# A Mamba-style block beside an FFN in fp32: W_out's columns one slot sooner, another list of sums handed over, the FFN's first output column in steps of 2, 4 and 5 tiles

## The chip, the cores and the metric

The kernel runs on one core of one Trainium2 chip. It is written in a low-level language in which each engine has its own instruction list in program order and waits on counting semaphores: PE (TensorE, matrix products), DVE (VectorE), ACT (ScalarE), POOL (GpSimd), and SP, which here only issues DMA transfers. The metric is the device time of one execution in microseconds. The time given for the kernel before is the median of three runs; the profile is one more execution with a time of its own.

## The reference

Four sequences (batches) of 512 tokens with 512 channels, all in fp32. A Mamba-style branch and a gated FFN read the same normed input, and their product is added to the input. With the scan's width D = 1024, N = 16 states for each channel, a step size of rank R = 32 and an FFN width of 1376:

```python
xn = _layernorm(x)
proj = xn @ W_in.T
u, gate = jnp.split(proj, 2, axis=-1)
u = silu(depthwise_causal_conv(u, conv_w) + conv_b)        # 4 taps
dt, Bm, Cm = jnp.split(u @ Wx.T, [R, R + N], axis=-1)      # each _rmsnorm'ed
delta = softplus(dt @ Wdt.T + dt_bias)
# for every token:
dA = exp(delta[..., None] * A)
state = dA * state + (delta * u)[..., None] * Bm[:, None, :]
y = einsum('bdn,bn->bd', state, Cm)
s = ((y + u * D_param) * silu(gate)) @ W_out.T
g = silu((silu(xn @ w_gate.T) * (xn @ w_up.T)) @ w_down.T)
out = x + s * g
```

## The kernel before

**Units and slots.** The four sequences run one after the other, b = 0 to 3. The scan of a sequence has 32 units, one for each state n and each half of the channels, and each unit two slots, so a sequence has 64 slots. In slot s:

- POOL makes dBu for two channel tiles, one product of 128x1024 (L913), up to three slots ahead of its reader;
- ACT makes two tiles of dA = exp(delta * A) (L673);
- DVE runs the two scans of 128x512 (L1191), and then adds into y the states of the unit before, weighted with C (L1107), two token tiles c in each slot: c = 0, 1 in an even slot, c = 2, 3 in an odd one;
- PE transposes the states of unit s // 2 (L1554, two token tiles, four blocks each) into two banks hT, as soon as the scans are done, then does a small transposition of other data where there is one, and then one column of matrix products.

A bank hT is free once the sum that reads it is made. DVE reads it itself (L1107), or the sum is handed over: ACT scales the tile (`take_state`, L779) and POOL adds it in (`add_part`, L866). `handed_over(u, first)` lists the tiles c given away for each unit u; `first` is True for sequence 0.

**Columns.** The columns of a sequence are laid out in tables by slot number. Slots 0 to 21 hold the FFN's gate and up projections (four slots sooner in sequences 1 to 3), then come the second half of W_in's gate, then, in sequences 1 to 3, the product with W_out of the sequence before: 8 columns from slot `S_OUT` on, two for each of the four output tiles e (L1464). The first of them waits for the gated values of this sequence (`sg_done`, DVE L1016), since its bank was the gate's. Two slots after each pair DVE multiplies with the FFN's result (`scale_g`, L1025), and from slot 32 on PE transposes these results back (L1372) and DVE adds them to the residual (L1152). From slot 31 on stand W_in's u columns of the next sequence (`U_AT`, L1252), and between them the FFN's down projection (`DOWN_AT`, L1498): four output tiles of 11 products t = 0 to 10 each, the first of them in three steps at slots 33, 36 and 39. fp32 products have two records for each t in the trace, so 8 records are four t.

**Loads.** SP loads the weights of L1464 and L1498 into a ring of two buffers, 512 KB at a time, in a fixed list that `load_order` makes: a buffer that is used up is loaded again when PE has signalled the last product that reads it (`dn_ps` after t = 3, 7 and 10). One buffer of w_down holds eight t. In sequence 0 the two buffers are still shared with W_in's u columns up to here, in the order U0, DOWN0, U0+1, DOWN0+1: DOWN0 (t = 0 to 7) and DOWN0+1 (t = 8 to 10 of tile 0, and on) lie in the same buffer. In sequences 1 and 2 they lie in the two buffers side by side. In sequence 3 the down projection has another form, which the change leaves alone.

**POOL's list.** Beside dBu and the handed sums POOL makes the step sizes delta (`step_size`, L843), the scan's inputs delta * u (`inputs`, L848, 128x1024 each), in sequence 0 the low parts of split weights (`rest_w`, L831, each waiting for ACT's rounding, L520), the powers of the norms (L815 and L826) and the products with the gate (L852). Each stands at a fixed slot. `inputs(b+1, 0)` of the next sequence waits for DVE's step sizes (L1177) and stands in slot 61, behind that slot's dBu and ahead of the one made in slot 62.

## Time and profile before

| | us |
|---|---|
| median of 3 runs (1109.97 to 1112.58) | 1111.97 |
| profiled execution | 1112.61 |
| its span | 1110.8 |
| PE busy | 1024.4 |
| DVE busy | 1035.5 |
| POOL busy | 967.4 |
| ACT busy | 719.0 |

The profiled execution is 0.64 us over the median. Its span runs from the first to the last instruction; 1.8 us lie outside it. The mean granted TensorE clock is 0.972 of full speed. In a timeline a row is: start, duration, engine, source line, operation, tiles written and read, sizes, and in brackets the idle time just before it with the engine whose work ended it. DVE's slot 0 of the four sequences starts at about 64, 335, 594 and 852 us.

### The profile page before, as it was taken

What the parts mean: (1) busy time and instruction counts of PE and PEld (TensorE: products, weight loads), DVE (VectorE), ACT (ScalarE), POOL (GpSimd) and SP (SyncE); (2) the same over time, 40 slices, a digit from 0 to 9 for tenths busy, and PEclk for the clock granted to TensorE, in tenths of its full rate; (3) what the DMA queues carried; (4) which work ended last, traced back from release to release, by engine and by line L of the source; (5) the groups of instructions that cost most, each with busy time, mean ns of one, the idle gap of its engine ahead of it and who ended that gap; (6) DMA issues with size and microseconds to landing.
All of it is one profiled execution on the core that took longest, in us unless ns stands there. A gap on an engine that the chain in (4) does not pass through costs nothing.

```text
span 1110.8 us, 14875 instructions
## 1 busy us (share of the span) xinstructions
PE 1024.4 (92%) x5040; PEld 753.5 (68%) x5040; DVE 1035.5 (93%) x1237; ACT 719.0 (65%) x1177; POOL 967.4 (87%) x531
## 2 busy tenths in 40 slices
PE   6969988899989999999999999998998999999877
PEld 5848766666758886675857887576766888555444
DVE  4679999899899999999999999999999999999995
ACT  4666766777576877477676786477576685456540
POOL 3648998999989999779979999968998999979981
PEclk9879999799989999999999999999999999999989
DMA  4626754443324654343233564334332543335511
GB/s 148 224 97 217 258 196 172 153 161 109 104 88 151 224 181 151 115 161 124 97 120 111 184 217 157 133 123 142 125 109 93 183 163 138 114 114 170 167 42 57
DMA packets 46619, 160.93 MB, mean 145 GB/s; under 512 B 5358, under 2 KB 5614, under 8 KB 37072
## 3 DMA queue, kind: packets, MB, share of 16 engines
q1 hardware_dynamic: 46400, 159.93, 42.2%
q8 instruction: 40, 0.66, 0.2%
q14 instruction: 35, 0.29, 0.1%
q10 hardware_dynamic: 144, 0.07, 0.0%
HBM read 135.59 MB, written 24.38 MB: 144 GB/s over the span
## 4 chain that ended last, share of the span: by engine, by line
PE 31%; POOL 28%; DVE 22%; issue 15%; ACT 3%; DMA 1%; SPq 0%; DVEq 0%; POOLq 0%
POOL sb_dBu L913 17%; DVE sb_h L1191 12%; PE pj L1252 10%; PE pj L1464 7%; PE hT L1554 6%; POOL sb_yT L866 6%; DVE sb_yT L1107 5%; DVE sb_un L989 2%; POOL sb_v L848 2%; PE pj L1572 2%; POOL sb_u L852 1%; PE pj L1498 1%; PE pj L1257 1%; PE pj L1529 1%; POOL sb_w_sp L831 1%
## 5 line engine op out<-in xcount | busy, mean ns | idle before, releaser
L913 POOL TENSOR_TENSOR sb_dBu<-sb_v,sb_bb 128x1024 f32<-128x1024 f32 x254 | 603.8, 2391 | 41.3 <-DVE sb_h L1191 28.5
L1191 DVE TENSOR_TENSOR_SCAN sb_h<-dA,sb_dBu 128x512 f32<-128x512 f32 x512 | 597.1, 1209 | 18.7 <-POOL sb_dBu L913 15.5
L673 ACT ACTIVATE dA<-sb_delta,sb_apar 128x512 f32<-128x512 f32 x510 | 344.9, 689 | 221.8 <-DVE sb_h L1191 219.9
L1252 PE MATMUL pj<-sb_x_hi,sb_w_sp 128*128 128x512 f32 x1208 | 344.6, 409 | 21.7 <-DVE sb_un L989 12.2
L1554 PEld LDWEIGHTS hT<-sb_ident,sb_h 128*128 128x128 f32 x2048 | 240.2, 144 | 127.3 <-issue 45.6
L1554 PE MATMUL hT<-sb_ident,sb_h 128*128 128x128 f32 x2048 | 283.5, 280 | 43.8 <-DVE sb_yT L1107 35.1
L1252 PEld LDWEIGHTS pj<-sb_x_hi,sb_w_sp 128*128 128x128 f32 x1208 | 223.2, 193 | 69.7 <-DVE sb_un L989 8.7
L1107 DVE SCALAR_TENSOR_TENSOR sb_yT<-hT,sb_cs,sb_yT 128x512 f32<-128x512 f32 x336 | 238.6, 735 | 10.0 <-PE hT L1554 9.4
L866 POOL TENSOR_TENSOR sb_yT<-sb_yT,sb_part 128x512 f32<-128x512 f32 x140 | 181.1, 1293 | 25.3 <-ACT sb_part L779 25.3
L1252 PE MATMUL pj<-sb_x_lo,sb_w_sp 128*128 128x512 f32 x604 | 167.3, 400 | 0.0
L779 ACT ACTIVATE sb_part<-hT,sb_cs_act 128x512 f32<-128x512 f32 x140 | 95.6, 683 | 95.4 <-PE hT L1554 85.3
L1252 PEld LDWEIGHTS pj<-sb_x_lo,sb_w_sp 128*128 128x128 f32 x604 | 117.1, 194 | 27.3
L1498 PE MATMUL pj<-sb_S,sb_ring 128*128 128x512 f32 x264 | 120.2, 593 | 0.0
L1464 PE MATMUL pj<-sb_u,sb_ring 128*128 128x512 f32 x192 | 86.6, 594 | 0.0
L1498 PEld LDWEIGHTS pj<-sb_S,sb_ring 128*128 128x128 f32 x264 | 47.9, 190 | 43.5 <-issue 43.0
L989 DVE SCALAR_TENSOR_TENSOR sb_un<-pj,sb_cw,sb_un 128x511 f32<-128x511 f32 (+2 forms) x93 | 69.5, 747 | 4.9 <-ACT sb_un L549 2.7
L831 POOL TENSOR_TENSOR sb_w_sp<-sb_ring,sb_w_sp 128x1024 fp32r<-128x1024 f32 x21 | 49.9, 2380 | 25.5 <-ACT sb_w_sp L520 25.3
L1464 PEld LDWEIGHTS pj<-sb_u,sb_ring 128*128 128x128 f32 x192 | 34.7, 191 | 35.0 <-issue 35.0
L852 POOL TENSOR_TENSOR sb_u<-sb_u,sb_sgate 128x512 f32<-128x512 f32 x32 | 41.1, 1288 | 8.5 <-DVE sb_u L1022 8.5
L848 POOL TENSOR_TENSOR sb_v<-sb_delta,sb_un 128x1024 f32<-128x1024 f32 x14 | 33.5, 2395 | 14.8 <-DVE sb_delta L1177 14.8
L1529 PE MATMUL pj<-sb_ring,sb_S 128*128 128x512 f32 x88 | 39.8, 593 | 0.0
L837 POOL TENSOR_TENSOR sb_un<-sb_v,sb_un 128x512 f32<-128x512 f32 x30 | 38.5, 1289 | 0.0
(148 smaller groups left out, 774.4 us busy)
## 6 DMA issues: line engine op xcount, KB each, us to landing
sb_w_sp<-w_cache SPq DMA_DIRECT2D x55, 1024.0 KB, 4.8
sb_ring<-w_ring SPq DMA_DIRECT2D x67, 512.0 KB, 3.6
sb_bb<-b_rows SPq DMA_DIRECT2D x128, 256.0 KB, 3.4
w_cache<-sb_w_sp SPq DMA_DIRECT2D x19, 1024.0 KB, 4.9
sb_xio<-x SPq DMA_DIRECT2D x7, 1024.0 KB, 7.6
out<-sb_xio SPq DMA_DIRECT2D x3, 1024.0 KB, 5.6
sb_xio<-x SPq DMA_DIRECT2D x4, 256.0 KB, 3.3
out<-sb_xio SPq DMA_DIRECT2D x4, 256.0 KB, 2.0
```

The lines of the kernel that those rows point to most:

```text
L673: nc.scalar.activation(dA[g % 2][:, :], delta[:, j, :], ACT.Exp, scale=apar[:, j, n:n + 1]).then_inc(dA_done, 1)
L779: nc.scalar.activation(dst, hT[c % H_BANKS][:, :], ACT.Copy, scale=cs_act[:, c, n:n + 1]).then_inc(ev_done, 1)
L831: nc.gpsimd.tensor_tensor(w_lo[:, buf], ring[:, slot], w_hi[:, buf].bitcast(fp32), ALU.subtract).then_inc(lo_done, 1)
L866: nc.gpsimd.tensor_tensor(y, y, part[:, (len(acts) - q) % 2, :], ALU.add).then_inc(yp_done, 1)
L913: nc.gpsimd.tensor_tensor(dBu[:, dbu_buffer(s), :, :], v[:, j:j + 2, :], bb[:, i % B_RING, :].unsqueeze(1).to_broadcast([P, 2, T]), ALU.mu ...
L989: nc.vector.scalar_tensor_tensor(out=acc[:, k:T], in0=bank[:, 0:T - k], scalar=cw[:, j, KC - 1 - k:KC - k], in1=acc[:, k:T], op0=ALU.mult, ...
L1107: nc.vector.scalar_tensor_tensor(out=y, in0=hT[c % H_BANKS][:, :], scalar=cn, in1=y, op0=ALU.mult, op1=ALU.add).then_inc(y_done, 1)
L1191: nc.vector.tensor_tensor_scan(h[:, i % 2, 2 * part + e, :], dA[g % 2][:, :], dBu[:, dbu_buffer(s), e, :], 0.0, ALU.mult, ALU.add).then_in ...
L1252: done = nc.tensor.matmul(bank[:, :], w[:, kk * P:(kk + 1) * P], xs[:, kk, :], start=(p == 0), stop=(p == len(products) - 1))
L1464: done = nc.tensor.matmul(pj[e % 2][:, :], ring[:, slot_of(b, OUT0 + e), part, m * P:(m + 1) * P], u[:, j, :], start=(j == 0), stop=(j == ...
L1498: done = nc.tensor.matmul(pj[DOWN_BANK[e]][:, :], ring[:, slot_of(b, DOWN0 + x3 // 2), x3 % 2, t % 4 * P:(t % 4 + 1) * P], S[:, t, :], sta ...
L1554: done = nc.tensor.transpose(hT[c % H_BANKS][:, j * P:(j + 1) * P], h[:, i % 2, j, c * P:(c + 1) * P], ident[:, :])
```

## The change

Four tables and the list of POOL are altered; no instruction is computed otherwise.

```diff
-S_OUT = 23
+S_OUT = 22
-DOWN_AT = {33: (0, range(0, 4)), 36: (0, range(4, 8)), 39: (0, range(8, 11)),
+DOWN_AT = {33: (0, range(0, 2)), 36: (0, range(2, 6)), 39: (0, range(6, 11)),
...
-        return () if u < FIRST_UNIT else (0, 2) if 11 <= u < 23 else (0,)
+        return () if u < FIRST_UNIT else (0, 2) if u < 21 else (0,)
+    if u in (17, 18):
+        return 0, 1, 2
...
-        after["used", OUT0] = "xres"
+        after["used", OUT0 + 1] = "xres"
...
-                    if s == 14:
+                    if s == (17 if first else 14):
                         step_size(b, 2)
-                    if s == 16:
+                    if s == (23 if first else 16):
                         inputs(b, 2)
-                    if s == 18:
+                    if s == (25 if first else 18):
                         step_size(b, 3)
-                    if s == 20:
+                    if s == (27 if first else 20):
                         inputs(b, 3)
...
-                    if s == SLOTS - 3:
+                    if s == SLOTS - 2:
                         inputs(b + 1, 0)
```

The eight W_out columns stand in slots 22 to 29 instead of 23 to 30, `scale_g` in slots 26, 28, 30 and 32. In sequence 0 the sums (21, 2) and (22, 2) go back to DVE, in its slots 45 and 47. In sequences 1 to 3 the sums (17, 1) and (18, 1) are handed over as well, out of DVE's slots 36 and 38. The load of the residual is issued behind the second W_out buffer's reload instead of the first's. POOL makes the second half's step sizes and inputs of sequence 0 later, and the first inputs of the next sequence behind the dBu of slot 62 (in the same slot) instead of ahead of it. Up to line 83 the numbers are alike; behind that they are 2 or 3 higher in the changed kernel.

On PE in sequence 0, slot 39, before: the transpositions of the states (L1554), of y (L1328), then the three products t = 8 to 10, the first of which waits for its weights (w_in0).

```order
390 L1554 MATMUL hT<-sb_ident,sb_h 128x128 [waits y_done]
391 L1554 MATMUL hT<-sb_ident,sb_h 128x128 x3
392 L1328 MATMUL pj<-sb_ident,sb_yT 128x128 [waits yu_done]
393 L1328 MATMUL pj<-sb_ident,sb_yT 128x128 x3
394 L1498 MATMUL pj<-sb_S,sb_ring 128x512 [waits w_in0]
395 L1498 MATMUL pj<-sb_S,sb_ring 128x512 x2
```

The same place in the changed kernel:

```order
390 L1557 MATMUL hT<-sb_ident,sb_h 128x128 [waits y_done]
391 L1557 MATMUL hT<-sb_ident,sb_h 128x128 x3
392 L1331 MATMUL pj<-sb_ident,sb_yT 128x128 [waits yu_done]
393 L1331 MATMUL pj<-sb_ident,sb_yT 128x128 x3
394 L1501 MATMUL pj<-sb_S,sb_ring 128x512 x2
395 L1501 MATMUL pj<-sb_S,sb_ring 128x512 [waits w_in0]
396 L1501 MATMUL pj<-sb_S,sb_ring 128x512 x2
```

The products t = 6 and 7 now stand right ahead of the three that wait for the next weights.

On SP around the same place, before: loads of B's rows (L384), of split weights (L444) and of the ring (L378); the ring's load is the one of DOWN0+1.

```order
71 L444 DMA sb_w_sp<-w_cache 128x2048 [waits u_ps,wc_out1,wc_out0]
72 L384 DMA sb_bb<-b_rows 128x512 [waits dBu_done]
73 L378 DMA sb_ring<-w_ring 128x1024 [waits dn_ps]
74 L384 DMA sb_bb<-b_rows 128x512 [waits dBu_done]
75 L444 DMA sb_w_sp<-w_cache 128x2048 [waits u_ps,wc_out1,wc_out0]
```

In the changed kernel:

```order
71 L446 DMA sb_w_sp<-w_cache 128x2048 [waits u_ps,wc_out1,wc_out0]
72 L386 DMA sb_bb<-b_rows 128x512 [waits dBu_done] x2
73 L446 DMA sb_w_sp<-w_cache 128x2048 [waits u_ps,wc_out1,wc_out0]
74 L380 DMA sb_ring<-w_ring 128x1024 [waits dn_ps]
75 L386 DMA sb_bb<-b_rows 128x512 [waits dBu_done]
```

The ring's load moved behind one load of B's rows and one of split weights.

On PE in sequence 1, slots 22 to 24, before: state transpositions (L1554), transpositions of the next sequence's x (L1228), and the first W_out columns (L1464).

```order
362 L1554 MATMUL hT<-sb_ident,sb_h 128x128 x8
363 L1228 MATMUL pj<-sb_ident,sb_xio 128x128 x8
364 L1554 MATMUL hT<-sb_ident,sb_h 128x128 x8
365 L1464 MATMUL pj<-sb_u,sb_ring 128x512 x4
366 L1554 MATMUL hT<-sb_ident,sb_h 128x128 x8
367 L1228 MATMUL pj<-sb_ident,sb_xio 128x128 x8
368 L1464 MATMUL pj<-sb_u,sb_ring 128x512 x4
```

In the changed kernel:

```order
362 L1557 MATMUL hT<-sb_ident,sb_h 128x128 x8
363 L1231 MATMUL pj<-sb_ident,sb_xio 128x128 x8
364 L1467 MATMUL pj<-sb_u,sb_ring 128x512 x4
365 L1557 MATMUL hT<-sb_ident,sb_h 128x128 x8
366 L1467 MATMUL pj<-sb_u,sb_ring 128x512 x4
367 L1557 MATMUL hT<-sb_ident,sb_h 128x128 x8
368 L1231 MATMUL pj<-sb_ident,sb_xio 128x128 x8
```

The first W_out column stands ahead of slot 23's state transpositions instead of behind them.

On POOL at the turn from sequence 0 to 1, before: dBu (L913), handed sums (L866), and the next sequence's inputs (L848).

```order
119 L866 TENSOR_TENSOR sb_yT<-sb_yT,sb_part 128x512
120 L913 TENSOR_TENSOR sb_dBu<-sb_v,sb_bb 128x1024
121 L848 TENSOR_TENSOR sb_v<-sb_delta,sb_un 128x1024
122 L913 TENSOR_TENSOR sb_dBu<-sb_v,sb_bb 128x1024
123 L866 TENSOR_TENSOR sb_yT<-sb_yT,sb_part 128x512
```

In the changed kernel:

```order
120 L868 TENSOR_TENSOR sb_yT<-sb_yT,sb_part 128x512
121 L915 TENSOR_TENSOR sb_dBu<-sb_v,sb_bb 128x1024 x2
122 L868 TENSOR_TENSOR sb_yT<-sb_yT,sb_part 128x512
123 L850 TENSOR_TENSOR sb_v<-sb_delta,sb_un 128x1024
124 L915 TENSOR_TENSOR sb_dBu<-sb_v,sb_bb 128x1024 x2
```

The inputs moved behind one dBu and one handed sum.

## Rows read from the trace of the kernel before

**Rows 1.** Page, part 1: busy us (share of the span) and instructions of each engine.

```profile
PE 1024.4 (92%) x5040; PEld 753.5 (68%) x5040; DVE 1035.5 (93%) x1237; ACT 719.0 (65%) x1177; POOL 967.4 (87%) x531
```

**Rows 2.** Page, part 5: costliest groups: busy, mean ns of one | idle before, releaser.

```profile
L913 POOL TENSOR_TENSOR sb_dBu<-sb_v,sb_bb 128x1024 f32<-128x1024 f32 x254 | 603.8, 2391 | 41.3 <-DVE sb_h L1191 28.5
L866 POOL TENSOR_TENSOR sb_yT<-sb_yT,sb_part 128x512 f32<-128x512 f32 x140 | 181.1, 1293 | 25.3 <-ACT sb_part L779 25.3
```

**Rows 3.** Waits, whole run: engine, tile, line <- releaser: us in total, times, longest.

```profile
PE hT L1554 <- DVE sb_yT L1107: 35.1, 28, 2.9
```

**Rows 4.** Timeline of DVE, sequence 0: slots 17 and 21.

```profile
139.29 2.34 DVE L1191 TENSOR_TENSOR_SCAN sb_h<-dA,sb_dBu 128x512 f32<-128x512 f32 x2 [0.92 <-POOL sb_dBu L913]
...
158.23 2.34 DVE L1191 TENSOR_TENSOR_SCAN sb_h<-dA,sb_dBu 128x512 f32<-128x512 f32 x2 [1.16 <-POOL sb_dBu L913]
```

**Rows 5.** Timeline of POOL, sequence 0: the dBu of slot 31.

```profile
189.72 2.36 POOL L913 TENSOR_TENSOR sb_dBu<-sb_v,sb_bb 128x1024 f32<-128x1024 f32 x1 [3.86 <-DVE sb_h L1191]
```

**Rows 6.** Timeline of DVE, sequence 0, slots 50 to 55.

```profile
280.62 2.34 DVE L1191 TENSOR_TENSOR_SCAN sb_h<-dA,sb_dBu 128x512 f32<-128x512 f32 x2 [1.84 <-POOL sb_dBu L913]
...
285.40 2.34 DVE L1191 TENSOR_TENSOR_SCAN sb_h<-dA,sb_dBu 128x512 f32<-128x512 f32 x2 [1.20 <-POOL sb_dBu L913]
...
300.89 2.34 DVE L1191 TENSOR_TENSOR_SCAN sb_h<-dA,sb_dBu 128x512 f32<-128x512 f32 x2 [0.62 <-ACT dA L673]
```

**Rows 7.** Timeline of PE, sequence 0, slots 39 and 40.

```profile
241.53 2.74 PE L1498 MATMUL pj<-sb_S,sb_ring 128*128 128x512 f32 x6
244.11 1.04 PE L1554 MATMUL hT<-sb_ident,sb_h 128*128 128x128 f32 x8
```

**Rows 8.** Line 378, 226 to 262 us: the ring's two loads, issue to landing.

```profile
DMA to landing us min/median/max: 3.5/3.6/3.7
```

**Rows 9.** Timeline of DVE, sequence 0, slot 41.

```profile
248.67 0.73 DVE L1107 SCALAR_TENSOR_TENSOR sb_yT<-hT,sb_cs,sb_yT 128x512 f32<-128x512 f32 x1
249.31 2.31 DVE L989 SCALAR_TENSOR_TENSOR sb_un<-pj,sb_cw,sb_un 128x511 f32<-128x511 f32 x3
```

**Rows 10.** Windows: stretch, busy us (instructions) of PE, PEld, DVE, ACT, POOL, then granted clock.

```profile
326.00:331.00 5.00, 5.00 (x16) 4.33 (x17) 4.37 (x6) 3.75 (x5) 5.00 (x3) 0.50 0.00 0
585.00:588.00 3.00, 3.00 (x11) 2.61 (x10) 2.35 (x3) 2.40 (x4) 3.00 (x3) 0.50 0.00 0
...
1022.00:1025.00 3.00, 1.38 (x12) 1.01 (x10) 3.00 (x5) 1.38 (x2) 3.00 (x3) 1.00 0.54 175
```

**Rows 11.** Timeline of PE at the turn to sequence 1.

```profile
325.95 1.94 PE L1554 MATMUL hT<-sb_ident,sb_h 128*128 128x128 f32 x8 [2.92 <-DVE sb_yT L1107]
...
342.42 1.07 PE L1252 MATMUL pj<-sb_x_hi,sb_w_sp 128*128 128x512 f32 x4
...
344.22 1.16 PE L1252 MATMUL pj<-sb_x_hi,sb_w_sp 128*128 128x512 f32 x4
```

**Rows 12.** Timeline of PE at the turn to sequence 3.

```profile
858.45 1.07 PE L1252 MATMUL pj<-sb_x_hi,sb_w_sp 128*128 128x512 f32 x4
...
861.15 1.16 PE L1252 MATMUL pj<-sb_x_hi,sb_w_sp 128*128 128x512 f32 x4 [0.28 <-DVE sb_S L1133]
```

**Rows 13.** Timeline of DVE at the turn to sequence 3.

```profile
856.52 2.34 DVE L1191 TENSOR_TENSOR_SCAN sb_h<-dA,sb_dBu 128x512 f32<-128x512 f32 x2 [0.68 <-POOL sb_dBu L913]
```

**Rows 14.** Timeline of PE, sequence 1, slots 23 and 24.

```profile
430.96 3.67 PE L1464 MATMUL pj<-sb_u,sb_ring 128*128 128x512 f32 x8
434.47 1.04 PE L1554 MATMUL hT<-sb_ident,sb_h 128*128 128x128 f32 x8
```

**Rows 15.** Timeline of DVE, sequence 1, slots 24 to 35.

```profile
430.19 0.68 DVE L1016 SCALAR_TENSOR_TENSOR sb_sgate<-sb_sgate,pj 128x512 f32<-128x512 f32 x1
...
433.08 0.72 DVE L1107 SCALAR_TENSOR_TENSOR sb_yT<-hT,sb_cs,sb_yT 128x512 f32<-128x512 f32 x1
...
474.71 0.69 DVE L1152 TENSOR_TENSOR sb_xio<-sb_xio,pj 128x512 f32<-128x512 f32 x1 [0.65 <-PE pj L1372]
```

**Rows 16.** Timeline of PE, sequence 3, slots 34 and 35.

```profile
986.02 0.66 PE L1372 MATMUL pj<-sb_ident,sb_gT 128*128 128x128 f32 x4 [1.29 <-DVE sb_xio L1152]
```

## The prediction, made before the changed kernel was run

> **What bounds the kernel now.** I read the busy shares first [rows 1]: DVE 93%, PE 92%, POOL 87%. No engine bounds the whole; the three hand buffers to one another, and whichever is last differs from slot to slot. The grouped waits come next [rows 3]: PE waits 35.1 us in 28 places for DVE's sums, since the banks hT are free only when DVE has read them. So a term of the change is worth what it moves at its own slot, minus what the next engine then says. The timelines of the slots that the change touches are the rest of the reading. All sums are made against the profiled execution, 1112.61 us, which is 0.64 over the median of the runs, 1111.97.
>
> **Sequence 0, POOL's list in the first half.** DVE waits for dBu in slots 17, 19 and 21; the first and the last are 0.92 and 1.16 us [rows 4]. The four moved operations are as large as a dBu (128x1024), 2.39 us each [rows 2]. With the first ones gone from slots 14 to 20, the three waits, about 3.1 us with the middle one taken as the mean, go. But the work has to be done before slot 32, and three of the four pieces, 7.2 us, now stand in slots 23 to 27. POOL's only idle time there is 3.86 us [rows 5]. The excess, 7.2 - 3.86 = 3.3 us, less the lead that DVE's earlier arrival doesn't leave it, returns as waits in slots 26 to 28. Followed row by row (dBu, rest of a split weight after ACT's rounding, a moved piece, in their new order) slot 29 starts 0.8 us sooner than now. Ends: 0 if POOL eats all of it, -3.1 if none. I take **-0.8**, as the excess is near the gain.
>
> **Sequence 0, two sums back to DVE.** POOL makes two additions of 1.29 us less [rows 2], 2.58 us, ahead of slots 50 and 51, where DVE waits 1.84 and 1.20 us for dBu, and ahead of slot 55, where it waits 0.62 us for ACT [rows 6], which in turn stands behind POOL's powers there. DVE takes over two sums; each moves its next instruction on by 0.64 us (248.67 to 249.31) [rows 9], 1.3 in all. The two waits are 3.04 us against POOL's 2.58 plus DVE's own 1.3 of delay, so both go. -3.04 - 0.62 + 1.3 = **-2.4**; ends -1.3 (only POOL's 2.58) and -2.4.
>
> **Sequence 0, steps of 2, 4 and 5 tiles.** The three products t = 8 to 10 begin at 241.53 [rows 7], with weights that were loaded when t = 7 in slot 36 had freed their buffer. The order shows that t = 7 is now the second product of slot 39, right ahead of t = 8, and that both buffers' loads are the same buffer. So t = 6 and 7 end at 241.53 + 2 x 0.91 = 243.4 (2.74 for three is 0.91 each [rows 7]); SP issues the load then and it lands 3.6 us later [rows 8], at 247.0; three products of 2.6 us follow, and the transpositions behind them, of which the first tile takes half of 1.04, are ready at 250.7. Their reader on DVE is the next slot's sum, now at 248.67 [rows 9]: a stall of **2.0 us**. PE idles 3.6 us for it. In the trace PE's granted clock is 0.50 for the 5 us from 326 and the 3 us from 585, both behind idle times of near 2.9 us [rows 10, 11], 1.2 in place of 2.4 GHz; at 1022 to 1025, where PE was idle half of the time in smaller pieces, it stayed 1.00 [rows 10]. An idle time of 3.6 is nearer to the first kind. Three us at half clock lose 1.5 us of work, five lose 2.5; the next columns in slots 40 to 44 are full ones with DVE close behind. I add 1.7, in all **+3.7**; ends +2.0 (clock stays) and +5.2. In sequences 1 and 2 the two buffers are loaded side by side, beforehand, and nothing happens.
>
> By the Trainium skill's page "DMA: Bandwidth & Descriptors" (Anatomy of one DMA) a transfer takes 2.0 us plus its bytes over 436 GB/s, which is 3.2 us for 512 KB as an estimate; the trace has 3.5 to 3.7 [rows 8], and by the page the stall would be 1.6 instead of 2.0. By "TensorE: Matmul & The Clock Gate" (Part 1) the array runs at half rate once it has sat idle and has to be busy again to get it back; the trace agrees behind both idle times of 2.9 us [rows 10, 11], and this speaks against the change, since a load in front of PE would then cost more than its wait.
>
> Sequence 0 together: -0.8 - 2.4 + 3.7 = **+0.5**.
>
> **The turns, inputs behind one dBu.** DVE waits 0.68 us for dBu in slot 1 before sequence 3 [rows 13] and as much in slot 62, because POOL's inputs, which wait for DVE, have the dBu of slot 62 behind them. With that dBu ahead these waits, 1.3 us at each of three turns, go. At the turn to sequence 1 nothing follows: PE is dense from 325.95 on, at half clock first, and its columns come 1.80 us apart (342.42 to 344.22) without idle time [rows 11]; DVE meets PE's transpositions again some ten slots on. At the turns to 2 and 3 PE's column waits for DVE's product with the FFN's gate: 858.45 to 861.15 is 2.70 us [rows 12], where a dense pair takes 1.80. So 0.9 to 1.0 comes back at each. I take **-0.95 twice, -1.9**; ends 0 and -1.3 for each.
>
> **W_out one slot sooner, sequences 1 and 2.** The first W_out column needs the gated values that DVE makes at 430.19 to 430.87 in slot 24 [rows 15], and begins at 430.96 already [rows 14]. One slot sooner in the list it can't begin sooner, but the transpositions of slot 23 now stand behind its 3.5 us instead of ahead of it. DVE's sum at 433.08 [rows 15] has to wait until the first tile is out at 434.47 + 1.04 = 435.5 [rows 14], 2.4 us. Followed slot by slot, DVE is 2.5 us late at slot 26, up to 4.9 at slots 31 and 33, and once the columns end a slot sooner 3.5 us come back in slot 30 and two of its own waits for PE vanish: the addition to the residual at 474.71 [rows 15] comes at 476.7. **+2.0**; ends +0.9 (PE has only one block of transpositions more to do behind 430.96, 434.47 to 435.35) and +2.7. From there DVE is last, and the two sums handed over in slots 36 and 38 save it 2 x 0.64 = **-1.3**; POOL has nothing to lose there. Net **+0.7** in each, +1.4.
>
> **Sequence 3.** The start of W_out is bound the same way and its last column ends where it does now. Behind it stand no columns of a next sequence: PE waits for DVE already, 1.29 us at 986.02 [rows 16]. DVE has one slot more to do between the last column and the residual, so the tail's down projection begins one DVE slot later, by 3.3 us. From there to about 1022 PE bounds. PE's idle time grows from 1.29 to about 3 us, again the kind behind which the clock fell [rows 10, 11]: between 0.3 and 3.4, I take +1.5. The handed sums save only 0.3 here. +3.3 + 1.5 - 0.3 = **+4.5**.
>
> **Sum.** 0.5 - 1.9 + 1.4 + 4.5 = +4.5; 1112.6 + 4.5 = **1117.1 us**.
>
> **Rivals.** (a) *No change: the clock holds.* All mechanisms as above, but behind neither idle time does the clock fall: the 1.7 and the 1.5 that I added for it go, 4.5 - 3.2 = +1.3, 1113.9 us. For it: smaller idle times at 1022 to 1025 left the clock at 1.00 [rows 10]. Against: both of 2.9 didn't. Chance 0.22. (b) *Faster: W_out's early column costs nothing.* If DVE's and PE's slack between slots 24 and 36 takes the 2.4 us in (DVE waits for PE there already, 0.65 at 474.71 [rows 15]), so that the column freed at slot 30 is a gain, S_OUT gives 0 in sequences 1 to 3: the sum loses 2.0 + 2.0 + 3.3 + 1.5 = 8.8 and gives -4.3, 1108.3 us; with the load's stall hidden too, -8.0, 1104.6 us. It decides at the point where slot 35's residual addition starts no later, relative to slot 24, than now. Against it: PE is dense from 430.96 to that place. Chance 0.12. (c) *Slower than forecast.* Both clocks stay down for the long spell and POOL's list gives nothing back: (5.2 - 3.7) + (3.4 - 1.5) + 0.8 = 4.2 more, 1121.3 us. Chance 0.16. My own case, within 1.5 us of 1117.1, has 0.5.
>
> **How the numbers follow.** 0.3% of 1112 is 3.3 us, about what a measurement of this kernel can tell from no change. Faster by more than that is case (b), 0.12. Slower by more is my case for nearly all of it, 0.42, and (c), less a little for offsetting errors: 0.55. The rest, 0.33, is (a) and the lower edge of mine. The range takes (a), mine and nearly all of (c), and reaches to the slower part of (b): 1109.5 to 1121.5 us.
>
> **What would show it.** In the changed profile: DVE's waits for POOL at slots 17, 19, 21, 50, 51 and at the three turns gone; a PE idle time of some 3.6 us before the third product of slot 39 in sequence 0, released by a ring load, and a granted clock of 0.50 behind it; in sequences 1 and 2 a DVE wait of about 2.4 us for hT in slot 25, and the residual's additions 2 us later relative to the first W_out column; in sequence 3 the tail's down projection 3.3 us later behind that column. I am wrong if the ring's load lands before t = 8 needs it, if the first W_out column begins sooner than DVE's gate in slot 24 (then S_OUT is a gain), or if DVE has slack in the slots 24 to 35 that I took for none.

## The result, and the profile after

| | before | changed |
|---|---|---|
| median, us | 1112.58 (7 runs, 1105.41 to 1114.66) | 1118.18 (7 runs, 1116.82 to 1120.68) |
| profiled execution, its span | 1112.61, 1110.8 | 1118.18, 1116.4 |
| mean granted clock | 0.972 | 0.972 |

The ratio is 1.0058 with a 95% interval of 1.004 to 1.0076: 0.6% slower, clear of no change. The forecast was 1117.1 us in a range of 1109.5 to 1121.5, with slower as the likeliest case at 0.55.

The page of the changed kernel, part 1 (the busy shares, as [rows 1]), and three of the grouped waits of the whole run (the first answers to [rows 3]):

```profile
PE 1023.5 (92%) x5040; PEld 752.9 (67%) x5040; DVE 1033.0 (93%) x1233; ACT 718.9 (64%) x1181; POOL 972.6 (87%) x535
```

```profile
PE hT L1557 <- DVE sb_yT L1110: 34.3, 23, 2.9
...
DVE sb_yT L1110 <- PE hT L1557: 26.4, 24, 4.9
...
DVE sb_h L1194 <- POOL sb_dBu L915: 8.3, 10, 1.5
```

The engines do the same work but for a few sums that changed hands between DVE and POOL. What changed is who waits: before, DVE waited 15.5 us in 18 places for POOL's dBu, the idle time that page part 5 lists ahead of the scans, and 9.4 us for PE's transpositions. Now it is 8.3 us for POOL and 26.4 us for PE, with one wait of 4.9 us. So 7 us were taken off POOL's account and 17 put on PE's.

How much of it reached the end is read from the start of DVE's scans slot by slot, changed minus before. This difference is called the lag (positive is later). Behind slot 4 of sequence 0 it moves at these places, and elsewhere by 0.2 us or less:

| place | lag goes from, to | moved | forecast |
|---|---|---|---|
| sequence 0, slots 16 to 29 (POOL's list) | 0.0, -1.0 | -1.0 | -0.8 |
| sequence 0, slots 42 to 43 (steps 2, 4, 5) | -1.0, +4.0 | +5.0 | +3.7 |
| sequence 0, slots 43 to 55 (two sums to DVE) | +4.0, +1.3 | -2.7 | -2.4 |
| turn to sequence 1 | +1.5, 0.0 | -1.5 | 0 |
| sequence 1, slots 25 to 36 (W_out) | 0.0, +2.3 | +2.3 | +2.0 |
| sequence 1, slots 36 to 39 (handed sums) | +2.3, +0.9 | -1.3 | -1.3 |
| turn to sequence 2 | +0.9, -0.1 | -1.0 | -0.95 |
| sequence 2, slots 25 to 39 | -0.1, +0.8 | +0.9 | +0.7 |
| turn to sequence 3 | +0.8, -0.7 | -1.5 | -0.95 |
| sequence 3, slots 25 to 40 (W_out, sums) | -0.7, +2.8 | +3.5 | +4.5 |
| sequence 3, slots 40 to 51 | +2.8, +4.1 | +1.3 | none |
| sequence 3, slot 51 to the end | +4.1, +5.6 | +1.5 | none |

**Sequence 0, slot 39.** PE's timeline of the changed kernel, then SP's:

```profile
240.53 1.88 PE L1501 MATMUL pj<-sb_S,sb_ring 128*128 128x512 f32 x4
246.05 5.49 PE L1501 MATMUL pj<-sb_S,sb_ring 128*128 128x512 f32 x6 [3.63 <-DMA sb_ring<-w_ring]
251.33 1.25 PE L1557 MATMUL hT<-sb_ident,sb_h 128*128 128x128 f32 x8
```

```profile
239.48 0.32 SPq L446 DMA_DIRECT2D sb_w_sp<-w_cache  x1
242.45 0.33 SPq L380 DMA_DIRECT2D sb_ring<-w_ring  x1
```

The load is issued when t = 7 is done (242.4) and PE stands still for 3.63 us until it lands; the forecast had 3.6. The three products then take 5.49 us, where they took 2.74 before [rows 7]: the clock. The same place by windows (busy us of PE, PEld, DVE, ACT and POOL, then the granted clock):

```profile
246.00:249.00 3.00, 2.95 (x4) 1.41 (x5) 1.72 (x2) 0.00 (x0) 3.00 (x2) 0.50 0.16 59
249.00:252.00 3.00, 3.00 (x8) 1.34 (x8) 0.00 (x0) 0.00 (x0) 0.26 (x1) 0.54 0.00 0
252.00:255.00 3.00, 3.00 (x18) 2.54 (x17) 2.32 (x4) 2.82 (x5) 2.06 (x2) 1.00 0.00 0
```

1.2 in place of 2.4 GHz for nearly 6 us, and DVE stands idle for 4.9 us of it: its sum, at 248.67 before [rows 9], has this wait in DVE's timeline:

```profile
252.61 0.76 DVE L1110 SCALAR_TENSOR_TENSOR sb_yT<-hT,sb_cs,sb_yT 128x512 f32<-128x512 f32 x1 [4.90 <-PE hT L1557]
```

**Sequence 1, slots 22 to 25.** PE's and DVE's timelines of the changed kernel, to be held against [rows 14, 15]:

```profile
427.38 1.04 PE L1231 MATMUL pj<-sb_ident,sb_xio 128*128 128x128 f32 x8
430.91 3.67 PE L1467 MATMUL pj<-sb_u,sb_ring 128*128 128x512 f32 x8 [2.49 <-issue]
434.42 1.04 PE L1557 MATMUL hT<-sb_ident,sb_h 128*128 128x128 f32 x8
435.29 3.60 PE L1467 MATMUL pj<-sb_u,sb_ring 128*128 128x512 f32 x8
```

```profile
430.13 0.68 DVE L1019 SCALAR_TENSOR_TENSOR sb_sgate<-sb_sgate,pj 128x512 f32<-128x512 f32 x1
...
435.49 0.75 DVE L1110 SCALAR_TENSOR_TENSOR sb_yT<-hT,sb_cs,sb_yT 128x512 f32<-128x512 f32 x1 [2.39 <-PE hT L1557]
```

The first W_out column begins at 430.91, behind DVE's gate (430.13 + 0.68), as it did before at 430.96. It is put down to "issue", but it is that gate: the column follows it by 0.1 us in both kernels. PE stands idle for 2.49 us ahead of it with slot 23's transpositions behind it in its list, and DVE waits 2.39 us for them (2.4 in the forecast).

**The turns.** DVE's wait for dBu at 856.52 [rows 13] is gone, and PE's column at the turn to sequence 3, at 861.15 before [rows 12], is here:

```profile
858.39 1.07 PE L1255 MATMUL pj<-sb_x_hi,sb_w_sp 128*128 128x512 f32 x4
859.30 1.03 PE L1557 MATMUL hT<-sb_ident,sb_h 128*128 128x128 f32 x8
860.39 1.17 PE L1255 MATMUL pj<-sb_x_hi,sb_w_sp 128*128 128x512 f32 x4
```

858.39 to 860.39 is 2.00 us, before it was 2.70.

**Sequence 3, slots 34 to 36.** PE's timeline: the state transpositions that now wait for a DVE sum, and the first column of the tail's down projection, which began at 986.52 before:

```profile
985.45 1.79 PE L1557 MATMUL hT<-sb_ident,sb_h 128*128 128x128 f32 x8 [2.92 <-DVE sb_yT L1110]
...
989.76 3.60 PE L1532 MATMUL pj<-sb_ring,sb_S 128*128 128x512 f32 x8
```

It begins 3.2 us later although the last W_out column begins 0.7 us sooner (976.33, before 977.06), so it is 4.0 us later behind that column. The forecast had 3.3 us and up to 3.4 for the clock.

**Sequence 3, slot 51.** DVE's timeline has a wait there that the kernel before didn't have:

```profile
1045.75 2.34 DVE L1194 TENSOR_TENSOR_SCAN sb_h<-dA,sb_dBu 128x512 f32<-128x512 f32 x2 [1.22 <-POOL sb_dBu L915]
```

### The profile page after: what moved, and what is told of

The parts are those of the page before. It is cut to its first block, busy times and chain, and to the rows that moved or that the text cites. A ratio compares the mean times of both kernels' runs of the same rounds, so it can differ in the third digit from the quotient of the medians.

```text
span 1116.4 us, 14880 instructions
## 1 busy us (share of the span) xinstructions
PE 1023.5 (92%) x5040; PEld 752.9 (67%) x5040; DVE 1033.0 (93%) x1233; ACT 718.9 (64%) x1181; POOL 972.6 (87%) x535
## 4 chain that ended last, share of the span: by engine, by line
PE 55%; DVE 23%; issue 11%; POOL 8%; ACT 2%; DMA 1%; SPq 0%; DVEq 0%; POOLq 0%; ACTq 0%
PE pj L1255 26%; PE hT L1557 12%; DVE sb_h L1194 12%; PE pj L1467 7%; DVE sb_yT L1110 5%; POOL sb_dBu L915 4%; PE pj L1501 3%; DVE sb_un L992 3%; PE pj L1575 2%; POOL sb_yT L868 2%; PE pj L1260 2%; POOL sb_w_sp L833 1%; PE pj L1597 1%; DVE sb_u L1025 1%; PE pj L1331 1%
## 5 line engine op out<-in xcount | busy, mean ns | idle before, releaser
L1110 DVE SCALAR_TENSOR_TENSOR sb_yT<-hT,sb_cs,sb_yT 128x512 f32<-128x512 f32 x332 | 235.6, 735 | 27.2 <-PE hT L1557 26.4
L868 POOL TENSOR_TENSOR sb_yT<-sb_yT,sb_part 128x512 f32<-128x512 f32 x144 | 185.0, 1287 | 25.8 <-ACT sb_part L781 25.8
L1501 PE MATMUL pj<-sb_S,sb_ring 128*128 128x512 f32 x264 | 123.1, 604 | 3.6 <-DMA sb_ring<-w_ring 3.6
```

Of the source, the lines that this page charges most:

```text
L868: nc.gpsimd.tensor_tensor(y, y, part[:, (len(acts) - q) % 2, :], ALU.add).then_inc(yp_done, 1)
L1110: nc.vector.scalar_tensor_tensor(out=y, in0=hT[c % H_BANKS][:, :], scalar=cn, in1=y, op0=ALU.mult, op1=ALU.add).then_inc(y_done, 1)
L1501: done = nc.tensor.matmul(pj[DOWN_BANK[e]][:, :], ring[:, slot_of(b, DOWN0 + x3 // 2), x3 % 2, t % 4 * P:(t % 4 + 1) * P], S[:, t, :], sta ...
```

## The experiments

Twelve kernels were run. "Lag" is always DVE's scan start against the kernel before, slot by slot as in the table above. Only its moves from one slot to another are used, so that the start of the program, which differs by up to 6 us from one execution to the next, drops out. W_out's columns and the steps were run alone and taken out alone. POOL's list, the two sums of sequence 0 and the turns were never run alone: their terms are told apart by the place at which the lag moves, and in the two kernels that keep all three as they were (W_out alone, steps alone) DVE's waits at those places are about as long as before.

**W_out back in its old slots**, and with it the load of the residual, which goes back behind the first reload in every kernel that has W_out in slots 23 to 30.

```diff
-S_OUT = 22
+S_OUT = 23
```

> The changed kernel with only W_out's columns put back into slots 23 to 30 (and the residual's load behind the first reload, as before). Theory: the early column can't begin before DVE's gate of slot 24, so the transpositions of slot 23 queue behind it; in the changed profile that cost 2.3 us in each of sequences 1 and 2 up to slot 36, and 3.5 us in sequence 3. Undone, the three losses go: about 8 us less than the changed kernel, -2.5 us against the kernel before (+5.6 - 8.1), ratio near 0.998; DVE's wait of 2.4 us for hT in slot 25 is gone. Rival: the loss in these slots comes from the handed sums or the residual's load, then the time stays near +5 us and the wait stays.

Measured: 1107.81 us, ratio 0.9963 (0.995 to 0.9975). In sequences 1 and 2 the lag stays flat from slot 9 to 36, DVE's wait in slot 25 is gone, and the two handed sums then give 1.3 us in each. In sequence 3 it loses 1.7 us at slots 26 to 28 instead of 3.5: the clock was at 0.57 from 942 to 945 us in this execution, around the first W_out column. In the medians the kernel is 10.4 us faster than the changed one. W_out accounts for 2.3 us in each of sequences 1 and 2 and the difference of 3.5 and 1.7 in sequence 3, which is more than the 5.6 us that the whole change costs; a shorter half clock behind the stall of slot 39 (3.6 instead of 5.0 us) and in the tail is in the 10.4 too.

**One slot sooner, alone on the kernel before.**

```diff
-S_OUT = 23
+S_OUT = 22
```

> The kernel before with one part of the change alone: W_out's columns in slots 22 to 29 (and the residual's load behind the second reload). Theory: the loss doesn't need the other parts. DVE waits about 2.4 us for hT in slot 25 of sequences 1 and 2, slot 36 starts 2.3 us later relative to slot 25, nothing of it comes back since DVE has no wait for POOL between slot 36 and the turn, but the turn's two waits for POOL (0.65 and 0.70) can take nothing in either, as they move along; sequence 3 is 3.5 us longer to slot 34 and keeps it. In all +8 us, ratio 1.0072. Rival (the early column is harmless by itself, the handed sums or POOL's list made it late): under +2 us.

Measured: 1123.58 us, ratio 1.0118 (1.0089 to 1.0146), more than I expected. Sequence 1 loses 2.2 us, sequence 3 3.5 up to slot 34, both as expected. In sequence 2 it is 3.9. PE's timeline there:

```profile
691.53 5.37 PE L1464 MATMUL pj<-sb_u,sb_ring 128*128 128x512 f32 x8 [2.50 <-issue]
696.73 1.04 PE L1554 MATMUL hT<-sb_ident,sb_h 128*128 128x128 f32 x8
```

The idle time of 2.50 us is the one of 2.49 in the changed kernel's sequence 1. There the column behind it took 3.67 us at full clock, here 5.37 at a granted clock of 0.66 (691 to 694). The early column costs 2.3 us, or 3.9 when the clock falls behind it. Of the 18 early first columns in the six kernels with W_out in slots 22 to 29, four ran at half clock (5.2 to 5.4 us); in the changed kernel's profile none did. No wait of DVE for the residual's load shows in this kernel.

**The first column behind slot 23's transpositions.** W_out's first two columns are issued together in slot 23.

```diff
-                    e, part = (s - S_OUT) // 2, (s - S_OUT) % 2
-                    if 0 <= e < KH and not first:
+                    for q in () if s == S_OUT else (0, 1) if s == S_OUT + 1 else (s - S_OUT,):
+                        e, part = q // 2, q % 2
...
```

> The changed kernel, but W_out's first column is issued in slot 23, behind that slot's transpositions and ahead of the second column; the other columns stay in slots 24 to 29. Theory (the loss in sequences 1 and 2 starts with slot 23's transpositions queueing behind a column that itself waits for DVE): DVE's wait in slot 25 is gone, slot 26 is late by 0.5 to 0.9 us instead of 2.4, and slot 36 by 1.4 instead of 2.3. In sequence 3 the loss is of another kind (DVE has one slot more to do between the last column and the residual) and stays at 3 to 3.5 us up to slot 34. In all 2 to 2.5 us less than the changed kernel, ratio 1.003 to 1.004. Rival (it is PE's total work behind DVE's gate that counts, not its order): slot 36 stays 2.3 us late.

Measured: 1113.02 us, ratio 1.0011 (0.9988 to 1.0034), 5 us less than the changed kernel where 2 to 2.5 were expected. Up to slot 36 of sequences 1 and 2 it is as expected: no wait in slot 25, slot 26 not late at all, 1.1 us of wait for hT in slot 26, and slot 36 late by 1.4. The lag at slot 34 of sequence 3 grows by 2.7 us. So the order gives back 0.9 us in each sequence. The rest of the gain isn't one term: the profiled execution (1114.74) is only 3.4 us below the changed kernel's; in it the stall of sequence 0 cost 3.5 instead of 5.0, but POOL's list gave nothing (see the part on the prediction). The ten executions spread from 1108.39 to 1119.78, and what separates the median from them isn't explained. The cause of the loss in sequences 1 and 2 is the order, for 0.9 of the 2.3 us. That the other 1.4 are one slot's transpositions that PE has to fit in is my reading and not tested.

**Steps of 4, 4 and 3 again.**

```diff
-DOWN_AT = {33: (0, range(0, 2)), 36: (0, range(2, 6)), 39: (0, range(6, 11)),
+DOWN_AT = {33: (0, range(0, 4)), 36: (0, range(4, 8)), 39: (0, range(8, 11)),
```

> The changed kernel with only the steps of 4, 4 and 3 products put back. Theory: the wait of 3.6 us for the ring's load in sequence 0, slot 39, goes, with the half clock behind it: slot 43 starts 5.0 us sooner. Second question: in the changed profile DVE's waits for POOL in slots 50 and 51 were gone, and POOL had had the 5 us of the stall to run ahead. If the two additions taken from POOL suffice alone, slot 56 starts 5.0 us sooner too, +0.6 us against before in all; if it was the stall that let POOL catch up, 0.5 to 3 us of the waits at slots 50 and 51 come back, and the total is +1 to +3.5 us.

Measured: 1113.70 us, ratio 1.0019 (1.0 to 1.0038). The lag doesn't move between slots 42 and 43, and DVE's waits at slots 50 and 51 stay away: the lag falls by 2.5 us up to slot 55 (2.7 in the changed kernel). So the two sums taken from POOL suffice without the stall. In this execution too the first W_out column of sequence 2 ran at half clock (5.37 us) and cost 3.9 instead of 2.3.

**Steps of 2, 6 and 3.** `36: (0, range(2, 8))`, so that t = 6 and 7 are in slot 36.

> The changed kernel with steps of 2, 6 and 3 products: the first step is the changed one, but t = 6 and 7 are in slot 36. Theory (what counts is how long before t = 8 the product t = 7 is made, not the size of the first step): no wait for the ring's load, slot 43 as with 4, 4 and 3 within 0.5 us plus what the longer column of slot 36 costs (two products more, 1.8 us, of which DVE's wait in slots 37 and 38 takes 0 to 1.8). Rival (the load is late for another reason, behind the other loads that moved ahead of it): PE waits over 1 us for the load here too.

Measured: 1113.34 us, ratio 1.0014 (0.9995 to 1.0034), no wait for the load. PE's timeline:

```profile
221.86 5.32 PE L1501 MATMUL pj<-sb_S,sb_ring 128*128 128x512 f32 x12
...
236.46 2.74 PE L1501 MATMUL pj<-sb_S,sb_ring 128*128 128x512 f32 x6
```

The longer column costs nothing (the lag moves by 0.1 us or less from slot 36 to 43). It is the place of t = 7, not the size of the first step. (This execution is 0.7 us behind the one with steps of 4, 4 and 3 at slot 43, but it was so at slot 36 already, by a wait for ACT that two kernels with other steps have as well.)

**Steps of 2, 5 and 4.** `36: (0, range(2, 7))`, so that only t = 7 stands ahead of t = 8.

> The changed kernel with steps of 2, 5 and 4 products: only t = 7 and behind it t = 8 to 10 are in slot 39. Theory: t = 7 ends 0.9 us sooner than in the changed kernel, so the load is issued and lands 0.9 us sooner; PE's idle time in front of t = 8 is again 3.6 us, the clock falls again, and the stall to slot 43 is 5.0 - 0.9 = 4.1 us. If the clock doesn't fall this time it is 2.0 - 0.9 = 1.1 us. Rival (the load's landing time is set by the load of split weights ahead of it): it lands at the same time as in the changed kernel, the idle time grows to 4.5 us and the stall stays 5.0.

Measured: 1118.90 us, ratio 1.0055 (1.0041 to 1.0069); the stall to slot 43 is 3.3 us, smaller than both. Two things differ. The load is issued 2.1 us behind the load of split weights instead of 3.0, and it takes 4.0 us from issue (243.82) to the product (247.82): 0.4 of the 0.9 us is lost, in the direction of the rival. That it is lost behind the load of split weights is likely but not shown by one run. And the half clock was shorter. PE's timeline:

```profile
247.82 4.46 PE L1501 MATMUL pj<-sb_S,sb_ring 128*128 128x512 f32 x6 [4.04 <-DMA sb_ring<-w_ring]
```

4.46 for the three products, against 5.49 in the changed kernel and 2.74 at full clock.

**The steps alone on the kernel before.**

> The kernel before with one part alone: steps of 2, 4 and 5 products. Theory: the wait of 3.6 us for the ring's load appears in slot 39 of sequence 0, slot 43 starts 3.3 to 5.0 us later (the spread is the length of the half clock behind it). But POOL runs on meanwhile, and DVE's waits for it at slots 50 and 51 (1.84 and 1.20) are there to be taken in: 3.0 of it comes back, and the part alone costs only +0.3 to +2.0 us, ratio 1.0003 to 1.0018. So the parts don't add up: in the changed kernel the two sums given back to DVE had already used those waits. Rival (POOL is held up by the stall as DVE is): the waits stay and the cost is +3.3 to +5.0.

Measured: 1116.10 us, ratio 1.0029 (1.0009 to 1.0048). The stall is 3.6 us, and my theory fell: the waits for POOL stayed. DVE's timeline:

```profile
285.29 2.34 DVE L1191 TENSOR_TENSOR_SCAN sb_h<-dA,sb_dBu 128x512 f32<-128x512 f32 x2 [1.64 <-POOL sb_dBu L913]
...
290.07 2.34 DVE L1191 TENSOR_TENSOR_SCAN sb_h<-dA,sb_dBu 128x512 f32<-128x512 f32 x2 [1.20 <-POOL sb_dBu L913]
```

The rival was right: POOL is held up by the stall as DVE is. Its timeline:

```profile
253.91 1.30 POOL L866 TENSOR_TENSOR sb_yT<-sb_yT,sb_part 128x512 f32<-128x512 f32 x1 [2.18 <-ACT sb_part L779]
...
258.62 1.31 POOL L866 TENSOR_TENSOR sb_yT<-sb_yT,sb_part 128x512 f32<-128x512 f32 x1 [1.05 <-ACT sb_part L779]
```

The handed sums in POOL's list need a tile that ACT scales from a bank hT, which PE fills late, and POOL takes its list in order: it stood idle for 3.2 of the 3.6 us. It began the dBu of slot 43 11.9 us ahead of its scan (8.3 before), since that one stood ahead of the stalled sums, but the one of slot 46 9.1 against 8.8. The parts add up after all.

**Sums 17 and 18 back on DVE.** The two lines `if u in (17, 18): return 0, 1, 2` are taken out of the changed kernel.

> The changed kernel with the sums (17, 1) and (18, 1) of sequences 1 to 3 back on DVE. Theory: in sequences 1 and 2 DVE is last behind slot 36 and pays 0.65 us twice in each, +2.6 us. In sequence 3 POOL had only 2.5 us of lead at slot 51 before the change, so the 2.6 us of two more additions came back there as a DVE wait of 1.22 us: that wait is gone, and slot 51 stands 0 to 0.6 us sooner relative to slot 35 than in the changed kernel. In all +2.1 us against the changed kernel, ratio to before about 1.007. Rival: the wait at slot 51 comes from the shifted tail (S_OUT) and stays; then +3.3 us.

Measured: 1121.46 us, ratio 1.0081 (1.006 to 1.0102). The wait at slot 51 of sequence 3 is gone and the lag flat from 37 to 51, while sequences 1 and 2 no longer get their 1.3 us back. The median is 3.3 us over the changed kernel's, the rival's number, but the rival's mechanism (the wait stays) is refuted; in this execution the first W_out column of sequence 3 ran at half clock (5.22 us, 1.5 us more of lag) and the stall of slot 39 cost 3.9 instead of 5.0. DVE's timeline around slot 51:

```profile
1044.68 0.72 DVE L1108 SCALAR_TENSOR_TENSOR sb_yT<-hT,sb_cs,sb_yT 128x512 f32<-128x512 f32 x1
1045.33 2.33 DVE L1192 TENSOR_TENSOR_SCAN sb_h<-dA,sb_dBu 128x512 f32<-128x512 f32 x2
```

**Both parts back: W_out in slots 23 to 30, steps of 4, 4 and 3.**

> The changed kernel with W_out's columns back in slots 23 to 30 and the first output column back in steps of 4, 4 and 3; what is left are POOL's list, the inputs at the turns and the handed sums. Theory: the terms add up. From the runs before: sequence 0 gives -1.0 and -2.5, the turns -1.5 each less up to 0.6 of half clock, the handed sums -1.3 in sequences 1 and 2 and +0.6 in sequence 3: -8 us, near 1104.3 us, ratio 0.9925 (the run with only W_out back less its own stall of 3.6 us). Rival (DVE and PE take the gains back from one another once the stalls are out): -3 to -4 us, ratio 0.997.

Measured: 1105.24 us, ratio 0.9935 (0.991 to 0.9961). What is left of the change makes the kernel faster by 0.65%, near the 0.9925 expected; the rival's 0.997 lies outside the interval. From slot 4 of sequence 0 to slot 63 of sequence 3 the lag falls by 6.0 us in all; sequence 3 has given back 1.7 at slots 27 and 28 (the clock, as in the first run) and 1.3 at slot 51 by then.

**The same with sums 17 and 18 on DVE.**

> As the run before it (W_out and the steps back), and the sums (17, 1) and (18, 1) back on DVE too: only the changes to POOL's list, the turns and sequence 0's sums are left. Theory: +1.3 us in each of sequences 1 and 2, and in sequence 3 DVE's wait at slot 51 gone (-1.2) against 0.65 to 1.3 us more on DVE: +2.1 to +2.7 us against the run before it, ratio to the kernel before 0.9945.

Measured: 1105.48 us, ratio 0.9944 (0.9927 to 0.996). The expected 2.1 to 2.7 us more than the run before it didn't come: the medians differ by 0.2 us, and the two can't be told apart in time. In the traces it is 1.3 us twice against 1.2 at slot 51 and a spell of half clock more or less.

**The same with sums 27 and 28 handed over instead.**

```diff
-    if u in (17, 18):
-        return 0, 1, 2
+    if u in (27, 28):
+        return 0, 1
```

> W_out and the steps back, and instead of (17, 1) and (18, 1) the sums (27, 1) and (28, 1) are handed over in sequences 1 to 3 (DVE's slots 56 and 58, POOL's 58 and 60), where POOL stood idle for 4.9 us in slots 60 and 61 in the kernel before. Theory (a handed sum is free where POOL has idle time before its next use): the same 1.3 us in each of sequences 1 and 2, and no wait at slot 51 of sequence 3: 1 to 1.5 us less than with 17 and 18, near 1103 us. Rival: POOL's inputs at the turn come late behind the added sums and DVE waits in slots 62 or 1; then equal or worse.

Measured: 1106.76 us, ratio 0.9941 (0.9919 to 0.9962), no gain. No wait at slot 51, but new ones in slots 57 (0.8 us) and 59 (1.0 us) of sequences 1 and 2, more than the 1.3 us that the handed sums save. They aren't POOL's. The one of slot 59:

```profile
564.16 2.34 DVE L1194 TENSOR_TENSOR_SCAN sb_h<-dA,sb_dBu 128x512 f32<-128x512 f32 x2 [0.99 <-ACT dA L675]
```

I had looked at POOL's idle time only. A handed sum is also 0.68 us on ACT, which makes dA and has no idle time ahead of slot 59 (softplus of the next sequence and a table load).

**POOL's last two pieces later still**, on top of both parts back.

```diff
-                    if s == (25 if first else 18):
+                    if s == (27 if first else 18):
                         step_size(b, 3)
-                    if s == (27 if first else 20):
+                    if s == (29 if first else 20):
                         inputs(b, 3)
```

> As the run with W_out and the steps back (the fastest so far), and of POOL's four moved pieces in sequence 0 the last two go later still: the step sizes of pair 3 from slot 25 to 27, its inputs from 27 to 29. In that run DVE waited 1.25 and 0.43 us for dBu in slots 26 and 27, while POOL stood idle in slots 28 to 30. Theory (the pieces only have to avoid the slots in which POOL has no lead): both waits go or shrink to under 0.5 together, and slot 31 starts 1.0 to 1.7 us sooner relative to slot 16, about 1 us less in all, ratio near 0.9925. Rival (the work returns wherever it stands ahead of slot 32): equal waits come back in slots 29 to 33 and nothing is gained.

Measured: 1103.43 us, ratio 0.9906 (0.9881 to 0.9932), the lowest median of all; the interval overlaps that of the kernel without this step, so the gain rests on the trace. The waits of 1.25 and 0.43 in slots 26 and 27 are gone; 0.9 us of them comes back in slot 34 (2.46 where it was 1.5). From slot 16 to 35 the lag falls by 2.3 us, against 1.0 in the changed kernel and in the one with both parts back. DVE's timeline:

```profile
206.93 2.34 DVE L1194 TENSOR_TENSOR_SCAN sb_h<-dA,sb_dBu 128x512 f32<-128x512 f32 x2 [2.46 <-POOL sb_dBu L915]
```

## Why the prediction was right, and where it wasn't

The sign and the size (+4.5 forecast, +5.6 in the profiled executions and in the medians) held, and so did the mechanisms of the parts but for the steps named below. Point by point:

- **POOL's list, -0.8: -1.0.** DVE's waits for POOL in slots 17, 19 and 21 [rows 4] went, and 1.24 + 0.42 us came back in slots 26 and 27, since the work went into slots where POOL's lead was already short. Moving two pieces by two slots more lowered the whole term by another 1.3 us. The prediction left out that PE waits for POOL here too. POOL's split weights are later by the moved pieces, and PE stands idle before them:

```profile
179.16 1.32 PE L1255 MATMUL pj<-sb_x_hi,sb_w_sp 128*128 128x512 f32 x4 [3.45 <-POOL sb_w_sp L833]
```

  In the kernel before the same column starts without idle time:

```profile
179.18 1.16 PE L1252 MATMUL pj<-sb_x_hi,sb_w_sp 128*128 128x512 f32 x4
```

  The idle time of 3.44 to 3.48 us is in all ten kernels with the pieces in slots 25 and 27; with them two slots later it is 1.2 us. A spell of half clock comes with it in all ten, and in none of the other four kernels. In eight of them DVE then waits 0.4 us for PE in slot 28, and the term is -1.0 at slot 29. In two (steps of 2, 5 and 4; the first column behind slot 23's transpositions) the half clock lasted twice as long, DVE waited 1.60 us, and the term was +0.2, nothing gained, as in rival (c). DVE's timeline with steps of 2, 5 and 4:

```profile
186.57 1.41 DVE L1110 SCALAR_TENSOR_TENSOR sb_yT<-hT,sb_cs,sb_yT 128x512 f32<-128x512 f32 x2 [1.60 <-PE hT L1557]
```

- **Two sums to DVE, -2.4: -2.7.** The three waits of [rows 6] went, shown without the stall too, though never by the two sums alone.
- **Steps of 2, 4 and 5, +3.7: +5.0.** The mechanism is shown from both sides (2, 6 and 3 has no stall; the steps alone have it). The idle time was 3.63 for 3.6. Mis-sized was the clock term: 1.7 forecast, 2.75 here (5.49 - 2.74) and 0.2 more in the transpositions, 1.5 with the steps alone (4.28 for the three products). The 2.0 us without the clock are right, but not as written: 243.4 + 3.6 + 2.6 and half of 1.04 would be 250.1 and a stall of 1.5. The 250.7 contains all of the 1.04, and so it is in the traces: with the steps alone DVE's sum starts 1.07 us behind the first transposition (252.51, 253.58). My range for the whole, +2.0 to +5.2, held it in every run: 3.3 to 5.0. (The load took 3.6 us from issue. The fit of the Trainium skill's page "DMA: Bandwidth & Descriptors" (Anatomy of one DMA) that the prediction set beside it is given there for transfers that GpSimd issues, and SP issues this one.)
- **The turns, -1.9: -4.0.** The step that failed is "at the turn to sequence 1 nothing follows". I let DVE meet a PE chain that ran at half clock for 5.5 us from 325.95 on. In the changed kernel the half clock began with the same idle time (2.87 us) but was over at about 330.5, so PE was no longer last and the 1.5 us that DVE gains at each turn (forecast 1.3) stayed:

```profile
327.43 1.94 PE L1557 MATMUL hT<-sb_ident,sb_h 128*128 128x128 f32 x8 [2.87 <-DVE sb_yT L1110]
329.02 1.75 PE L1255 MATMUL pj<-sb_x_hi,sb_w_sp 128*128 128x512 f32 x4
330.61 1.09 PE L1255 MATMUL pj<-sb_x_lo,sb_w_sp 128*128 128x512 f32 x4
```

  In the other runs 0.0 to 0.6 us of it came back at each turn, up to slot 9, the more the later the half clock ended, and in one turn all but 0.1. That was the turn to sequence 3 of the last run, where the clock was at 0.50 from 832 to 838 us: the long spell that the forecast took from the kernel before. So its mechanism is right for that spell. At the turn to sequence 3 of the changed kernel the clock stayed full, and the 1.5 us stayed as well (forecast 0.95). The full 1.5 is the bound, and the clock decides how much of it stays.
- **W_out in sequences 1 and 2, +2.0: +2.3**, and the handed sums -1.3: -1.3. The first is shown by taking it out and by doing it alone, and 0.9 us of it by the order alone.
- **Sequence 3, +4.5: +6.3.** Of it +3.5 up to slot 40 is the forecast mechanism. The clock did fall, to 0.60 in the window 985 to 988, but the down projection came 4.0 us later behind W_out, which leaves 0.7 us for the clock over the 3.3, where I had put 1.5. The step that failed is "POOL has nothing to lose there". It holds in sequences 1 and 2, where POOL begins the dBu of slot 51 3.8 us ahead of its scan. In sequence 3 it was 2.5, hardly more than the 2.39 that a dBu takes [rows 2], and two more additions of 1.29 us make it late: 1.22 us of wait, in every run with these sums and in none without them. The last 1.5 us are half clock in the tail: 0.50 to 0.74 from 1060 to 1069 and 0.53 from 1081 to 1084 us, under columns that DVE waits for (PE's column at 1064.67 takes 5.02 us, before it was 4.46). The kernel before had its spell from 1052 to 1062, mostly where PE has idle time. The largest piece, 1.3 us at slot 63, is in the six profiles that have a second spell of half clock in the tail and in none of the other eight. Why it falls where it does isn't settled.

The errors of the turns (-2.1) and of sequence 3 (+1.8) and of the stall (+1.3) partly cancelled; that the total was closer than its terms is luck. So is a part of the clock: the forecast priced no half clock behind PE's idle time at the first W_out column, and in the changed kernel's profile none came, but in four of the 18 such columns it cost another 1.5 to 1.7 us.

The clock terms rested on two idle times of 2.9 us that were both followed by half clock. That was too few. PE stands idle for 2.85 to 2.92 us at the same place of each of the three turns in all 14 profiles, and in nine of these 42 places the clock stayed full; at the turn to sequence 3 of the changed kernel it did:

```profile
843.63 1.22 PE L1557 MATMUL hT<-sb_ident,sb_h 128*128 128x128 f32 x8 [2.87 <-DVE sb_yT L1110]
844.88 1.17 PE L1255 MATMUL pj<-sb_x_hi,sb_w_sp 128*128 128x512 f32 x4
```

The rival "W_out's early column costs nothing" is refuted (1.0118 with that part alone), "the clock holds" too, for the stall: behind it the three products took 4.3 to 5.5 us in each of the six kernels that have it, 2.74 at full clock.

By the Trainium skill's page "TensorE: Matmul & The Clock Gate" (Part 1) the rate is one of two, set by how busy the array was of late. The windows agree on the two levels (0.50 and 1.00, with means between them where it changes within a window). In these runs the same 3.6 us of idle time cost 1.5 to 2.75 us on top of themselves.

## What to carry to other kernels

A column moved up in an in-order engine's list is not earlier if what it waits for isn't; what it does is to push back everything behind it, here the transpositions for another engine. Splitting work into steps by their size alone can put the last user of a buffer right ahead of the first user of its next content: look where the buffer is freed, not how the work is divided. Giving work to a neighbour needs the least lead that this neighbour has before its next deadline, for every engine that the handover passes (POOL in sequence 3, ACT in slot 59), not its busy share. And an engine whose list is made later has more than one reader: POOL's moved pieces spared DVE and made PE wait for its weights.

## What the runs showed of the hardware

- The same idle time of PE can be followed by full or by half clock. Ahead of the early W_out column it is 2.5 us in sequences 1 and 2 and 2.9 in sequence 3: the column behind it took 3.67 us (full clock) in 14 of 18 places and 5.2 to 5.4 us in four, for example 2.49 us and 3.67 in sequence 1 of the changed kernel, 2.50 and 5.37 in sequence 2 of the kernel with W_out's part alone. Behind 2.9 us at the turns the clock fell in 33 of 42 places. Behind 3.5 to 4.0 us ahead of t = 8 it fell in all six, but the three products took 4.28 to 5.49 us. A term for it can only be given as a range.
- The start of the program differs by up to 6 us between executions, in code that no kernel here changed (slot 0 starts at 59.8 to 66.1 us in the profiled ones), which is the size of the whole effect. The moves of the lag repeat to 0.1 us from kernel to kernel where the clock was the same, and differ by 1 us and more where it wasn't; the medians alone would have told little.
- A load of 512 KB took 3.5 to 3.6 us from issue to the product that waits for it when it was issued 3.0 us behind a load of 1 MB (five kernels), and 4.0 in the one kernel where it was issued 2.1 us behind it.
